# First attention: the key projection moved behind the output projection, PSUM banks reassigned, a head's weights split in two parts

## The chip, the cores and the metric

The kernel runs on one core of a Trainium2 chip. The metric is the time on the device in microseconds (us), lower is better. It is measured for the whole program, of which the part that the change touches is about two fifths.

## What is computed

The program computes two layers. Layer 0 is an attention with 32 query heads on 16 key heads (ALiBi bias, causal), times a gated network with experts; layer 1 is a recurrence, times an attention with experts. The change touches layer 0's attention alone:

```python
# x: 8 sequences of 512 tokens, 256 features; xn = layernorm(x)
qkv = inputs @ W_qkv                      # 32 query heads, 16 key and value heads of 64
k = jnp.repeat(k, NUM_QUERIES, axis=1)    # two query heads share a key head
scores = jnp.einsum('bhqd,bhkd->bhqk', q, k) / math.sqrt(HEAD_DIM)
scores = scores + bias[None]              # slope of the head times (key - query position)
scores = jnp.where(causal[None, None], scores, -jnp.inf)
attn = jax.nn.softmax(scores, axis=-1)
out = jnp.einsum('bhqk,bhkd->bhqd', attn, v)
return out.transpose(0, 2, 1, 3).reshape(B, S, Q_DIM) @ W_out
```

## The kernel before

`head_attention_phase` works in units. A unit is one key head with its two query heads on one sequence of 512 tokens; there are 16 heads of 8 sequences, 128 units, and they are numbered t, with head j outermost. Every engine has a program of its own, a loop over units written out by hand, and the programs meet through semaphores that count upward. Four blocks of 128 queries make up a unit; they are taken in the order 3, 0, 1, 2 and called 0 to 3 (`block_of`), so that step 0 has 512 keys, and steps 1, 2, 3 have 128, 256 and 384.

TensorE's `body(t)` (from L1060) is staggered over four units: it works on the scores of t+1, the turning (transposing) of the probabilities of t, the weighing of the values of t-1, and the projections of t+2. Its order is turn 0 (L1046), score 0 (L1034), turning of the values (L999), weighing (L1056), key and value projection of t+2 (L985), turns 1 and 2, scores 1 and 2, query projection of t+2 (L985), turn 3, score 3, and the output projection of t-1 (L1011) in two halves of three matmuls, m=1 and then m=0. The products are built from high and low parts, three terms each: high by high, low by high, high by low. A wait is put ahead of the last matmuls of the stage before (`last`, `late`), so that it is taken while others run.

There are eight PSUM banks: two for scores, two for turned probabilities, one for the weighed output, and three (`m_ps`) that the projections share. In body t with parity par, the keys and values go to bank par, the turned values of t+1 and then the queries of t+2 to bank 1-par, and the output projection's m=1 to bank 2 and m=0 to bank 1-par. So m=0 waits until VectorE's `q_rest` has read the queries there.

ScalarE takes the high parts out of PSUM (`take_k`, `take_v`, `take_q`, `take_o`), computes the exponentials (`exps`, L817) and copies half of each turned block (`turn_out`, L824). VectorE adds the bias and finds the maxima (`mask`, L902), inverts the sums (`invert`, L908), copies the other half (L914) and makes the low parts (`k_rest` L889, `values` L894, `q_rest` L882, `rest_o` L925); it sums the output into `acc` (`add_out`, L921), and at a head's last unit it makes the next head's two bias tiles (`set_bias`, L876). GpSimd scales the probabilities (`scale`, L769) and splits a head's raw weights in high and low part (`split`, L760 and L762). SP copies the keys to the other 64 partitions (`copy_k`, L712), and at a head's end issues a spill of x and the loads of the weights of the head after the next.

TensorE's loop runs over the 16 heads. In it stand two bodies, then an inner loop of two passes over two bodies, then two more bodies: six bodies of code for eight units. GpSimd's program is arranged likewise, with the split of the next head's weights ahead of the last two units.

Of the kernel before, what the change touches and what calls it, by code (L numbers as in the profile page):

```python
# [14 lines left out]
P = 128  # L15
B, S, D = 8, 512, 256
KT = D // P
TT = S // P
# [579 lines left out]
def head_attention_phase(nc, w_heads, wo_heads, slopes, ident, xh, xl, acc, xh_dram, xl_dram, row_sb, coef_sb,  # L598
# [9 lines left out]
    with ExitStack() as ctx:  # L608
# [57 lines left out]
        o_low = sem("at_o_low")  # L666
        zeroed = sem("at_zeroed")
        pool_ticks, dve_ticks, pe_ticks = sem("at_pool_ticks"), sem("at_dve_ticks"), sem("at_pe_ticks")
        block = ctx.enter_context(nc.Block())
# [18 lines left out]
        def kv_count(n):  # L688
            return n * 5 + (-3)

        def q_count(n):
            return n * 5 + (-2)

        def v_count(n):
            return n * 5 + 1

# [6 lines left out]
        def _(sp):  # L703
# [24 lines left out]
            with sp.Fori(0, KVH // 2) as jj:  # L728
                for jp in range(2):
                    j = jj * 2 + jp  # L730
                    with sp.Fori(0, PAIRS) as pair:
                        for par in range(2):
                            copy_k(kv_count(j * B + pair * 2 + (par + 2)), par)

                    to, half = ((xh_dram, xh), (xl_dram, xl))[jp]
                    sp.dma_start(to[:, :, ds(jj * S, S)], half[:, :, ds(jj * S, S)].bitcast(F32)).then_inc(spilled, 16)

                    sp.wait_ge(w_split, j + 1)
                    sp.wait_ge(wo_split, j + 1)
# [11 lines left out]
        def _(pool):  # L751
# [19 lines left out]
            def body(t):  # L771
                scale(t, 3)
                for j in range(3):
                    scale(t + 1, j)

            pool.wait_ge(w_loaded[0], 32)
            split(wh[:], wl[:], w_raw[0][:], 0).then_inc(w_split, 1)
            for j in range(3):
                scale(0, j)
            with pool.Fori(0, KVH // 2) as jj:  # L780
                for jp in range(2):
                    j = jj * 2 + jp
                    body(j * B)

                    pool.wait_ge(proj, j * (5 * B) + out_count(-1, 0))
                    wait_alone(pool, w_loaded[jp], jj * 32 + 32, pool_ticks)
                    split(woh[:], wol[:], wo_raw[jp][:], j * 2 + 1).then_inc(wo_split, 1)
                    body(j * B + 1)
                    with pool.Fori(1, PAIRS - 1) as pair:
                        for par in range(2):  # L790
                            body(j * B + pair * 2 + par)

                    pool.wait_ge(proj, j * (5 * B) + q_count(B - 1))
                    wait_alone(pool, w_loaded[1 - jp], (jj + jp) * 32 + 32, pool_ticks)
                    split(wh[:], wl[:], w_raw[1 - jp][:], j * 2 + 2).then_inc(w_split, 1)
                    body(j * B + (B - 2))
                    body(j * B + (B - 1))

        @block.scalar
        def _(act):  # L800
# [8 lines left out]

            def take_v(par):  # L810
                act.activation(vT[HD:P, :], m_ps[par][HD:P, :], ACT.Copy).then_inc(vT_out, 1)
# [21 lines left out]
            take_k(1, 0)  # L833
            take_v(0)
            take_q(2, 0)
            take_k(4, 1)
            take_v(1)
# [23 lines left out]
        def _(dve):  # L861
# [30 lines left out]
            def values(count, par):  # L892
                dve.wait_ge(proj, count)
                dve.tensor_copy(v[par][:].rearrange("p i d -> p (i d)"), m_ps[par][:, 0:TT * HD])\  # L894
                    .then_inc(proj_out, 1)
# [31 lines left out]
            def body(t, par, b_before, new_head=None):  # L927
# [19 lines left out]
                q_rest(t + 2, par)  # L947
# [3 lines left out]
                invert(t + 1, 2)  # L951
                add_out(t + (-1), 1 - par, b_before, 1)
                add_out(t + (-1), 1 - par, b_before, 0)

# [18 lines left out]
            for m in (1, 0):  # L973
                add_out(KVH * B - 1, 1, B - 1, m, skipped=3)

        @block.tensor
        def _(pe):
# [15 lines left out]
            def project_kv(n, par, b, last):  # L993
                project(m_ps[par], P, b, last)

            def turn_v(n, par):

                for i in range(TT):
                    ins = pe.transpose(m_ps[par][:, HD * i:HD * i + HD], vT[HD:P, P * i:P * i + P], ident[HD:P, HD:P])  # L999
                ins.then_inc(proj, 1)  # L1000

            def project_out(n, par, bank_free, last):

                for m in (1, 0):
# [3 lines left out]
                    for i, (w, o) in enumerate([(woh, oh), (wol, oh), (woh, ol)]):  # L1008
                        if m == 0 and i == 2:
                            last()  # L1010
                        ins = pe.matmul(bank[:], w[:, m * P:m * P + P], o[par][:], start=(i == 0), stop=(i == 2))  # L1011
                    ins.then_inc(proj, 1)
# [46 lines left out]

            def body(t, half, par, b_next, new_head=None, new_out=None):  # L1060

                def pair_turnable():
                    turnable(t, 1, 3)
                    pe.wait_ge(proj_out, v_count(t + 1))

                def next_turnable():
                    turnable(t, 3, 4)
                    pe.wait_ge(o_low, t + 1)

# [8 lines left out]
                if new_head is not None:  # L1078

                    pe.wait_ge(w_split, new_head + 1)  # L1080
# [12 lines left out]

            pe.wait_ge(zeroed, 1)
            pe.wait_ge(w_split, 1)
            project(m_ps[0], P, 0)
            project(m_ps[1], 0, 0)
            values_free(0)
            pe.wait_ge(proj_out, 1)
# [22 lines left out]
            pe.wait_ge(o_low, KVH * B + 1)  # L1122
            project_out(KVH * B - 1, 1, lambda: (pe.wait_ge(proj_out, 5 * KVH * B + 5), pe.wait_ge(vT_out, KVH * B + 2)), lambda: None)


# [1754 lines left out]
```

## Time and profile before

| | us |
|---|---|
| median of 3 runs | 3462.16 (3461.97 to 3463.49) |
| the profiled execution | 3461.67 |
| its span, first to last instruction | 3459.7 |
| of it, the first attention | about 62 to 1510 |

Busy time of the engines over the whole span: TensorE's matmuls 3203.6 us (93%), its weight loads 2347.7 (68%), VectorE 2336.1 (68%), ScalarE 2063.6 (60%), GpSimd 1184.1 (34%). The page has the engines' busy share in 40 slices, the DMA queues, and the costliest groups of instructions by line. A matmul's row gives its start and a modelled end that overlaps the next one, so that stages of TensorE are best measured from start to start. PE is TensorE, PEld its weight loads, DVE is VectorE, ACT is ScalarE, POOL is GpSimd. Register, branch and semaphore instructions have no rows.

### The profile page before, as it was taken

Reading aid. Unit: us, or ns where it says so; the run is one execution under the profiler, and the core shown is the slowest. Engines: PE = TensorE matmul, PEld = TensorE weight load, DVE = VectorE, ACT = ScalarE, POOL = GpSimd, SP = SyncE. Lnnn points to the kernel's source line nnn. Section 1 sums busy time; section 2 is a strip of 40 time slices with the busy share of each in tenths; the row PEclk is TensorE's granted clock in tenths of the full one; section 3 lists DMA queues with packets and bytes.
Section 4 is the critical chain, followed back from the end, with each engine's and each line's share of the span. In section 5 each row is a group of like instructions: output and inputs, shape, how many; then the busy total and the mean of one; then the engine's idle time right before and its main releaser. Section 6 shows DMA issues by size and latency. Waiting matters only on the chain. (4 is left out here: it accounts for less than half of the span.)

```text
span 3459.7 us, 72480 instructions
## 1 busy us (share of the span) xinstructions
PE 3203.6 (93%) x22702; PEld 2347.7 (68%) x22702; DVE 2336.1 (68%) x6854; ACT 2063.6 (60%) x4947; POOL 1184.1 (34%) x1820
## 2 busy tenths in 40 slices
PE   4999999999999999989999979879999964999995
PEld 3666666666666666668888855546666654888884
DVE  5788877877888788876666645556666625666665
ACT  4777777777777777765655543236566621555553
POOL 4444434443443344443333320042322202334432
PEclk9999999999999999999999989979999966999998
DMA  2111111111111111143433331101111134445545
GB/s 86 36 32 35 34 26 30 35 35 35 32 35 35 35 33 34 35 142 122 134 124 120 127 115 56 56 19 28 32 26 28 27 122 149 119 126 142 128 121 164
DMA packets 165548, 246.35 MB, mean 71 GB/s; under 512 B 30770, under 2 KB 115506, under 8 KB 165426
## 3 DMA queue, kind: packets, MB, share of 16 engines
q1 hardware_dynamic: 150834, 224.85, 21.2%
q0 software_dynamic: 14592, 19.93, 3.5%
q8 instruction: 69, 1.13, 0.1%
q14 instruction: 53, 0.43, 0.0%
HBM read 159.79 MB, written 41.16 MB: 58 GB/s over the span
## 5 line engine op out<-in xcount | busy, mean ns | idle before, releaser
L769 POOL TENSOR_SCALAR at_p<-at_p,at_recip 128x512 f32<-128x512 f32 (+3 forms) x1030 | 534.4, 535 | 865.5 <-DVE at_recip L908 865.5
L817 ACT ACTIVATE at_p<-at_p,at_nmax 128x512 f32<-128x512 f32 (+3 forms) x1032 | 571.6, 557 | 247.1 <-DVE at_nmax L902 235.8
L902 DVE CUSTOM_DVE_ANT_0 at_p<-at_s_ps,at_bias 128x512 f32<-128x512 f32 (+3 forms) x1032 | 449.1, 479 | 3.6 <-PE at_s_ps L1034 3.5
L1878 DVE CUSTOM_DVE_ANT_0 aa_a_ps<-aa_a_ps,aa_hidden 128x128 f32<-128x128 f32 (+3 forms) x512 | 247.3, 507 | 176.1 <-PE aa_a_ps L2042 172.9
L1034 PE MATMUL at_s_ps<-at_k_twice,at_q 64*128 64x512 f32 (+3 forms) x3096 | 343.4, 340 | 3.3 <-DVE at_nmax L902 3.3
L1056 PE MATMUL at_o_ps<-at_pT,at_v 128*64 128x512 f32 (+3 forms) x2064 | 307.5, 440 | 0.0
L1778 ACT ACTIVATE aa_pT<-aa_b_ps 128x512 f32<-128x512 f32 (+1 forms) x384 | 196.6, 529 | 178.8 <-PE aa_b_ps L2060 176.1
L1046 PEld LDWEIGHTS at_t_ps<-ident,at_p 64*128 64x128 f32 x5120 | 191.0, 138 | 143.2 <-issue 143.2
L914 DVE COPY at_pT<-at_t_ps 128x512 f32<-128x512 f32 (+3 forms) x512 | 235.9, 479 | 47.1 <-PE at_t_ps L1046 44.9
L526 DVE SCALAR_TENSOR_TENSOR nw_hl<-nw_h,nw_coef_now,nw_hh 128x512 fp32r<-128x512 f32 x192 | 149.9, 781 | 162.4 <-ACT nw_hh L454 162.4
L449 ACT ACTIVATE nw_h<-nw_h_ps,nw_b 128x512 f32<-128x512 f32 x192 | 132.2, 688 | 211.1 <-PE nw_h_ps L553 210.7
L1046 PE MATMUL at_t_ps<-ident,at_p 64*128 64x64 f32 x5120 | 241.7, 230 | 4.1 <-POOL at_p L769 3.2
L1056 PEld LDWEIGHTS at_o_ps<-at_pT,at_v 128*64 128x64 f32 x2064 | 137.0, 137 | 148.3 <-issue 121.1
L1034 PEld LDWEIGHTS at_s_ps<-at_k_twice,at_q 64*128 64x128 f32 x3096 | 226.7, 189 | 9.1 <-DVE at_nmax L902 3.9
L2593 POOL DMA_INDIRECT moe_dram<-ex_o,places x76 | 124.8, 1642 | 304.2 <-ACT ex_o L2620 212.1
L391 POOL TENSOR_SCALAR nw_w1h<-nw_w_raw 128x256 fp32r<-128x256 f32 x192 | 104.2, 543 | 324.1 <-PE nw_o_ps L568 318.4
L824 ACT ACTIVATE at_pT<-at_t_ps 128x512 f32<-128x512 f32 (+3 forms) x512 | 207.6, 431 | 2.4 <-PE at_t_ps L1046 2.3
L2042 PE MATMUL aa_a_ps<-aa_k,aa_q 128*128 128x128 f32 (+3 forms) x512 | 191.9, 387 | 14.9 <-DVE aa_nmax L1878 11.8
L985 PE MATMUL at_m_ps<-xh,at_wh 128*128 128x512 f32 (+1 forms) x520 | 189.5, 445 | 13.0 <-POOL at_wl L762 11.9
L817 ACT ACTIVATION_READ_ACCUMULATOR at_p<-at_p,at_nmax 128x1 f32 x1032 | 195.5, 189 | 0.0
L2632 ACT ACTIVATE ex_act<-ex_a_ps 128x512 f32<-128x512 f32 x114 | 68.1, 597 | 185.9 <-PE ex_b_ps L2728 185.9
L2685 DVE TENSOR_TENSOR ex_hid<-ex_act,ex_b_ps 128x512 f32<-128x512 f32 x114 | 78.5, 688 | 135.8 <-ACT ex_act L2632 134.6
(317 smaller groups left out, 8029.8 us busy)
## 6 DMA issues: line engine op xcount, KB each, us to landing
w_raw<-in_w_dram SPq DMA_DIRECT2D x57, 768.0 KB, 5.8
at_k_twice<-at_k_twice SPq DMA_DIRECT2D x130, 256.0 KB, 2.8
nw_w_raw<-in_w_all_dram SPq DMA_DIRECT2D x26, 1024.0 KB, 5.0
nw_w_raw<-in_w_all_dram SPq DMA_DIRECT2D x52, 512.0 KB, 6.9
nw_xh<-xh_dram SPq DMA_DIRECT2D x10, 512.0 KB, 4.2
nw_xl<-xl_dram SPq DMA_DIRECT2D x10, 512.0 KB, 4.9
at_w_raw<-in_w_heads_dram SPq DMA_DIRECT2D x18, 256.0 KB, 3.8
nw_x<-in_x_dram SPq DMA_DIRECT2D x9, 512.0 KB, 5.9
```

The source lines that it names most:

```text
L769: pool.tensor_scalar(p, p, recip[:, u:u + 1], 1.0, ALU.mult, ALU.mult).then_inc(scaled, 1)
L817: act.activation(p_sb[:, u, 0:N], p_sb[:, u, 0:N], ACT.Exp, bias=nmax[:, u:u + 1], scale=-1.0, accum_out=total[:, u:u + 1]).then_inc(exped, 1)
L824: act.activation(pT[par][:, :, 0:qt + 1, qt * P + HD:qt * P + P], turned_half(1)[:, :, turned_at(j), :], ACT.Copy).then_inc(odd_out, 1)
L902: dve.tensor_tensor_reduce(out=p_sb[:, u, 0:N], in0=s_ps[u % 2][:, score_at(u // 2)], in1=bias[:, u % 2, S - N:S], scale=1.0, scalar=BIG, ...
L914: dve.tensor_copy(pT[par][:, :, 0:qt + 1, qt * P:qt * P + HD], turned_half(0)[:, :, turned_at(j), :])\
L985: ins = pe.matmul(bank[:], weight[:, k, w:w + P], x[:, k, ds(b * S, S)], start=(i == 0 and k == 0), stop=(i == 2 and k == KT - 1))
L1034: ins = pe.matmul(s_ps[h][:, score_at(j)], qst[par][rows, q, at], k_twice[par][rows, k, 0:N], start=(i == 0), stop=(i == 2))
L1046: ins = pe.transpose(turned_half(half)[:, h, turned_at(j).start + k, :], p_sb[rows, 2 * j + h, k * P:k * P + P], ident[rows, rows])
L1056: ins = pe.matmul(o_ps[HD * h:HD * h + HD, k * P:S], v[par][:, k, :], pT[par][:, h, k, k * P:S], start=(k == 0), stop=(k == TT - 1))
L1778: act.activation(pT[group_of(n, s) % 2][:, s % REP, piece * S:piece * S + N], b_ps[done % 3][:, 0:N], ACT.Exp, scale=-1.0)\
L1878: dve.tensor_tensor_reduce(out=a_ps[i % 2][:, 0:N], in0=a_ps[i % 2][:, 0:N], in1=hidden[:, S - N:S], scale=1.0, scalar=BIG, op0=ALU.add, o ...
L2042: pe.matmul(a_ps[i % 2][:, 0:N], q_all[n % 2][:, head // 2, N - P:N], k_all[n % 2][:, head % 2, g, 0:N], start=True, stop=True).then_inc(s ...
```

## The change

TensorE projects the keys and values three units ahead in place of two, and does it as the last stage of the body, directly behind the output projection; the weighing is followed by turn 1. One more such projection stands in the prologue. The banks are given out anew: the turned values go to bank 2, the output projection's m=0 to bank par (which ScalarE has emptied with `take_v`), and the keys and values of t+3 to bank 1-par behind the queries of t+2. ScalarE takes the keys first in its body and the values behind a wait of their own, for the values' turning. VectorE makes the keys' low part ahead of `values`, and the output's low part behind `invert(t + 1, 0)`. The next head's weights are split in two parts, keys and values first, queries a unit later, and the two users wait for one part each. TensorE's eight bodies of a head are written out in its loop, without an inner loop; GpSimd's inner loop has one body.

```diff
@@ counts
         def kv_count(n):
-            return n * 5 + (-3)
+            return n * 5 + (-4)
         def v_count(n):
-            return n * 5 + 1
+            return n * 5 + 2
@@ sync
-                    sp.wait_ge(w_split, j + 1)
+                    wait_alone(sp, w_split, 2 * j + 2, sp_ticks)
@@ gpsimd
+            def split_heads(raw, part, n):
+                at = slice(part * P, part * P + P)
+                split(wh[:, :, at], wl[:, :, at], raw[:, :, at], n).then_inc(w_split, 1)
...
-                    body(j * B + 1)
-                    with pool.Fori(1, PAIRS - 1) as pair:
-                        for par in range(2):
-                            body(j * B + pair * 2 + par)
-                    pool.wait_ge(proj, j * (5 * B) + q_count(B - 1))
+                    with pool.Fori(1, B - 3) as b:
+                        body(j * B + b)
+                    pool.wait_ge(proj, j * (5 * B) + kv_count(B - 1))
                     wait_alone(pool, w_loaded[1 - jp], (jj + jp) * 32 + 32, pool_ticks)
-                    split(wh[:], wl[:], w_raw[1 - jp][:], j * 2 + 2).then_inc(w_split, 1)
+                    split_heads(w_raw[1 - jp], 1, j * 3 + 3)
+                    body(j * B + (B - 3))
+                    wait_alone(pool, proj, j * (5 * B) + q_count(B - 1), pool_ticks)
+                    split_heads(w_raw[1 - jp], 0, j * 3 + 4)
                     body(j * B + (B - 2))
                     body(j * B + (B - 1))
@@ scalar
-            def take_v(par):
+            def take_v(count, par):
+                act.wait_ge(proj, count)
                 act.activation(vT[HD:P, :], m_ps[par][HD:P, :], ACT.Copy).then_inc(vT_out, 1)
...
+                    take_k(kv_count(t + 2), par)
                     turn_out(t, 0, par)
+                    take_v(v_count(t + 1), par)
                     exps(t + 1, 0)
                     exps(t + 1, 1)
                     take_o(t, 1 - par)
-                    take_k(kv_count(t + 2), par)
                     turn_out(t, 1, par)
                     turn_out(t, 2, par)
-                    take_v(par)
@@ vector
                 mask(t + 1, 1)
+                k_rest(t + 2, par)
                 dve.wait_ge(summed, t + 1)
                 values(v_count(t + 1), 1 - par)
-                rest_o(t, 1 - par)
-                k_rest(t + 2, par)
...
                 invert(t + 1, 0)
+                rest_o(t, 1 - par)
                 turn_out(t, 3, par)
@@ tensor
                 turn(0)
-                score(t + 1, 1 - par, 0, lambda: values_free(t + 1))
+                score(t + 1, 1 - par, 0, values_turnable)
                 turn_v(t + 1, 1 - par)
-                weigh(t + (-1), 1 - par, lambda: pe.wait_ge(proj_out, out_count(t + (-2), 0)))
-                project_kv(t + 2, par, b_next, pair_turnable)
+                weigh(t + (-1), 1 - par, lambda: turnable(t, 1, 3))
                 turn(1)
                 turn(2)
                 score(t + 1, 1 - par, 1)
                 score(t + 1, 1 - par, 2)
-                project_q(t + 2, par, b_next, next_turnable)
+                project_q(t + 2, par, (b + 2) % B, lambda: turnable(t, 3, 4))
                 turn(3)
                 score(t + 1, 1 - par, 3)
-                project_out(t + (-1), 1 - par, lambda: pe.wait_ge(proj_out, q_count(t + 2)), next_unit)
+                project_out(par, lambda: pe.wait_ge(o_low, t + 1), lambda: pe.wait_ge(vT_out, t + 3),
+                            lambda: pe.wait_ge(proj_out, q_count(t + 2)))
+                project_kv(t + 3, par, (b + 3) % B, next_unit)
...
             project(m_ps[1], P, 1)
-            pe.wait_ge(proj_out, 3)
             project(m_ps[0], 0, 1)
+            pe.wait_ge(proj_out, 5)
+            project(m_ps[0], P, 2)
...
             with pe.Fori(0, KVH) as j:
-                body(j * B, j * PAIRS, 0, 2)
-                body(j * B + 1, j * PAIRS, 1, 3, new_out=j)
-                with pe.Fori(1, PAIRS - 1) as pair:
-                    for par in range(2):
-                        body(j * B + pair * 2 + par, j * PAIRS + pair, par, pair * 2 + (par + 2))
-                body(j * B + (B - 2), j * PAIRS + (PAIRS - 1), 0, 0, new_head=j + 1)
-                body(j * B + (B - 1), j * PAIRS + (PAIRS - 1), 1, 1)
+                for b in range(B):
+                    body(j * B + b, j * PAIRS + b // 2, b % 2, b, j + 1 if b == B - 3 else None,
+                         j + 1 if b == B - 2 else None, j if b == 1 else None)
```

## Rows read from the trace of the kernel before

**Rows 1.** Busy time by engine in the first attention; columns in the header.
```profile
core 0: us, PE busy (x) PEld busy (x) DVE busy (x) ACT busy (x) POOL busy (x), PEclk, DMA share, GB/s
75.00:1490.00 1415.00, 1414.15 (x12946) 950.17 (x12946) 1132.45 (x3837) 1056.34 (x3046) 571.82 (x1076) 1.00 0.14 33
```

**Rows 2.** Who waited for whom there: us in total, times, longest.
```profile
PEld at_m_ps L1011 <- DVE at_q L882: 24.1, 113, 0.2
```

**Rows 3.** TensorE's matmuls in one unit by time: start, us, engine, line, tiles.
```profile
709.50 0.71 PE L1046 MATMUL at_t_ps<-ident,at_p 64*128 64x64 f32 x16
...
713.44 0.73 PE L985 MATMUL at_m_ps<-xh,at_wh 128*128 128x512 f32 x2
...
715.04 0.59 PE L1046 MATMUL at_t_ps<-ident,at_p 64*128 64x64 f32 x12
...
717.89 0.59 PE L1046 MATMUL at_t_ps<-ident,at_p 64*128 64x64 f32 x12
...
718.98 0.50 PE L1011 MATMUL at_m_ps<-at_oh,at_woh 128*128 128x512 f32 x1
719.32 0.40 PE L1011 MATMUL at_m_ps<-at_oh,at_wol 128*128 128x512 f32 x1
...
719.78 0.44 PE L1011 MATMUL at_m_ps<-at_oh,at_woh 128*128 128x512 f32 x1
720.06 0.40 PE L1011 MATMUL at_m_ps<-at_oh,at_wol 128*128 128x512 f32 x1
...
720.62 0.28 PE L1046 MATMUL at_t_ps<-ident,at_p 64*128 64x64 f32 x2
```

**Rows 4.** The values' turning, once a unit, at a head's steps.
```profile
699.69 0.40 PE L999 MATMUL at_m_ps<-ident,at_vT 64*128 64x64 f32 x4
...
733.04 0.40 PE L999 MATMUL at_m_ps<-ident,at_vT 64*128 64x64 f32 x4
...
744.29 0.40 PE L999 MATMUL at_m_ps<-ident,at_vT 64*128 64x64 f32 x4
...
777.64 0.40 PE L999 MATMUL at_m_ps<-ident,at_vT 64*128 64x64 f32 x4
...
788.85 0.34 PE L999 MATMUL at_m_ps<-ident,at_vT 64*128 64x64 f32 x3
```

**Rows 5.** Other engines in the unit of rows 3, by time.
```profile
715.15 0.59 ACT L808 ACTIVATE at_k_twice<-at_m_ps 64x512 fp32r<-64x512 f32 x1 [0.99 <-PE at_m_ps L985]
...
718.99 0.68 DVE L882 SCALAR_TENSOR_TENSOR at_q<-at_m_ps,at_q 128x512 fp32r<-128x512 f32 x1
...
720.68 1.27 DVE L921 TENSOR_TENSOR acc<-at_m_ps,acc 128x512 f32 x2
```

**Rows 6.** VectorE's bias tiles for a new head, by time.
```profile
1490.71 1.11 DVE L876 TENSOR_SCALAR at_bias<-at_rel,at_slope 128x512 f32<-128x512 f32 x2
```

**Rows 7.** The prologue, by time: first scores, and the low part of unit 1's queries.
```profile
62.32 0.96 PE L1034 MATMUL at_s_ps<-at_k_twice,at_q 64*128 64x512 f32 x6
...
63.06 0.69 DVE L882 SCALAR_TENSOR_TENSOR at_q<-at_m_ps,at_q 128x512 fp32r<-128x512 f32 x1 [0.72 <-ACT at_q L804]
```

**Rows 8.** Whole program, DMA queue of TensorE's code: packets, MB, share of 16 engines.
```profile
q8 instruction: 69, 1.13, 0.1%
```

**Rows 9.** The same queue, 75 to 165 us.
```profile
q8 instruction: 5, 0.08, 0.4%
```

**Rows 10.** All DMA queues, 165 to 1500 us.
```profile
q1 hardware_dynamic: 17638, 44.66, 13.9%
q14 instruction: 2, 0.02, 0.0%
```

**Rows 11.** Busy time by engine from 80 to 165 us; columns as in rows 1.
```profile
80.00:165.00 85.00, 85.00 (x794) 57.57 (x793) 68.73 (x235) 64.47 (x187) 34.58 (x66) 1.00 0.15 36
```

**Rows 12.** One packet of that queue, 80 to 90 us.
```profile
q8 instruction: 1, 0.02, 0.7%
```

**Rows 13.** DMA issues of the whole program: times, KB each, median us to landing.
```profile
at_wo_raw<-in_wo_heads_dram SPq DMA_DIRECT2D x18, 128.0 KB, 3.8
...
recip_dram<-aa_recip SPq DMA_DIRECT2D x32, 8.0 KB, 1.4
```

More of the change, by code:

```diff
@@ L667, in head_attention_phase @@
         zeroed = sem("at_zeroed")
+        sp_ticks = sem("at_sp_ticks")
         pool_ticks, dve_ticks, pe_ticks = sem("at_pool_ticks"), sem("at_dve_ticks"), sem("at_pe_ticks")
@@ L774, in body @@
                     scale(t + 1, j)
+            def split_heads(raw, part, n):
+                at = slice(part * P, part * P + P)
+                split(wh[:, :, at], wl[:, :, at], raw[:, :, at], n).then_inc(w_split, 1)
             pool.wait_ge(w_loaded[0], 32)
-            split(wh[:], wl[:], w_raw[0][:], 0).then_inc(w_split, 1)
+            for part in range(2):
+                split_heads(w_raw[0], part, part)
             for j in range(3):
@@ L786, in _ @@
                     wait_alone(pool, w_loaded[jp], jj * 32 + 32, pool_ticks)
-                    split(woh[:], wol[:], wo_raw[jp][:], j * 2 + 1).then_inc(wo_split, 1)
-                    body(j * B + 1)
-                    with pool.Fori(1, PAIRS - 1) as pair:
-                        for par in range(2):
-                            body(j * B + pair * 2 + par)
-                    pool.wait_ge(proj, j * (5 * B) + q_count(B - 1))
+                    split(woh[:], wol[:], wo_raw[jp][:], j * 3 + 2).then_inc(wo_split, 1)
+                    with pool.Fori(1, B - 3) as b:
+                        body(j * B + b)
+                    pool.wait_ge(proj, j * (5 * B) + kv_count(B - 1))
                     wait_alone(pool, w_loaded[1 - jp], (jj + jp) * 32 + 32, pool_ticks)
-                    split(wh[:], wl[:], w_raw[1 - jp][:], j * 2 + 2).then_inc(w_split, 1)
+                    split_heads(w_raw[1 - jp], 1, j * 3 + 3)
+                    body(j * B + (B - 3))
+                    wait_alone(pool, proj, j * (5 * B) + q_count(B - 1), pool_ticks)
+                    split_heads(w_raw[1 - jp], 0, j * 3 + 4)
                     body(j * B + (B - 2))
@@ L833, in _ @@
             take_k(1, 0)
-            take_v(0)
+            take_v(1, 0)
             take_q(2, 0)
             take_k(4, 1)
-            take_v(1)
+            take_v(4, 1)
             take_q(5, 1)
@@ L893, in values @@
                 dve.wait_ge(proj, count)
-                dve.tensor_copy(v[par][:].rearrange("p i d -> p (i d)"), m_ps[par][:, 0:TT * HD])\
+                dve.tensor_copy(v[par][:].rearrange("p i d -> p (i d)"), m_ps[2][:, 0:TT * HD])\
                     .then_inc(proj_out, 1)
@@ L951, in body @@
                 invert(t + 1, 2)
-                add_out(t + (-1), 1 - par, b_before, 1)
-                add_out(t + (-1), 1 - par, b_before, 0)
+                add_out(t + (-1), par, b_before, 1)
+                add_out(t + (-1), par, b_before, 0)
             set_bias(0, True, 2)
@@ L973, in _ @@
             for m in (1, 0):
-                add_out(KVH * B - 1, 1, B - 1, m, skipped=3)
+                add_out(KVH * B - 1, 0, B - 1, m, skipped=2)
         @block.tensor
@@ L993, in project_kv, with project_out @@
             def project_kv(n, par, b, last):
-                project(m_ps[par], P, b, last)
+                project(m_ps[1 - par], P, b, last)
             def turn_v(n, par):
                 for i in range(TT):
-                    ins = pe.transpose(m_ps[par][:, HD * i:HD * i + HD], vT[HD:P, P * i:P * i + P], ident[HD:P, HD:P])
+                    ins = pe.transpose(m_ps[2][:, HD * i:HD * i + HD], vT[HD:P, P * i:P * i + P], ident[HD:P, HD:P])
                 ins.then_inc(proj, 1)
-            def project_out(n, par, bank_free, last):
+            def project_out(par, o_ready, bank_free, last):
                 for m in (1, 0):
@@ L1008, in project_out @@
                     for i, (w, o) in enumerate([(woh, oh), (wol, oh), (woh, ol)]):
-                        if m == 0 and i == 2:
-                            last()
-                        ins = pe.matmul(bank[:], w[:, m * P:m * P + P], o[par][:], start=(i == 0), stop=(i == 2))
+                        if i == 2:
+                            (o_ready if m else last)()
+                        ins = pe.matmul(bank[:], w[:, m * P:m * P + P], o[1 - par][:], start=(i == 0), stop=(i == 2))
                     ins.then_inc(proj, 1)
@@ L1058, in weigh, with body, values_turnable @@
                 ins.then_inc(summed, 1)
[L1060 to L1068, printed above, removed]
+            def body(t, half, par, b, new_keys=None, new_queries=None, new_out=None):
+                def values_turnable():
+                    values_free(t + 1)
+                    pe.wait_ge(proj_out, out_count(t + (-2), 1))
                 def next_unit():
@@ L1074, in body @@
                 turn(0)
-                score(t + 1, 1 - par, 0, lambda: values_free(t + 1))
+                score(t + 1, 1 - par, 0, values_turnable)
                 turn_v(t + 1, 1 - par)
-                weigh(t + (-1), 1 - par, lambda: pe.wait_ge(proj_out, out_count(t + (-2), 0)))
-                if new_head is not None:
-                    pe.wait_ge(w_split, new_head + 1)
-                project_kv(t + 2, par, b_next, pair_turnable)
+                weigh(t + (-1), 1 - par, lambda: turnable(t, 1, 3))
                 turn(1)
@@ L1085, in body @@
                 score(t + 1, 1 - par, 2)
-                project_q(t + 2, par, b_next, next_turnable)
+                if new_queries is not None:
+                    pe.wait_ge(w_split, new_queries * 2 + 2)
+                project_q(t + 2, par, (b + 2) % B, lambda: turnable(t, 3, 4))
                 turn(3)
@@ L1091, in body @@
                     pe.wait_ge(wo_split, new_out + 1)
-                project_out(t + (-1), 1 - par, lambda: pe.wait_ge(proj_out, q_count(t + 2)), next_unit)
+                project_out(par, lambda: pe.wait_ge(o_low, t + 1), lambda: pe.wait_ge(vT_out, t + 3),
+                            lambda: pe.wait_ge(proj_out, q_count(t + 2)))
+                if new_keys is not None:
+                    pe.wait_ge(w_split, new_keys * 2 + 1)
+                project_kv(t + 3, par, (b + 3) % B, next_unit)
             pe.wait_ge(zeroed, 1)
-            pe.wait_ge(w_split, 1)
+            pe.wait_ge(w_split, 2)
             project(m_ps[0], P, 0)
@@ L1098, in _ @@
             values_free(0)
-            pe.wait_ge(proj_out, 1)
             turn_v(0, 0)
@@ L1113, in _ @@
             with pe.Fori(0, KVH) as j:
-                body(j * B, j * PAIRS, 0, 2)
-                body(j * B + 1, j * PAIRS, 1, 3, new_out=j)
-                with pe.Fori(1, PAIRS - 1) as pair:
-                    for par in range(2):
-                        body(j * B + pair * 2 + par, j * PAIRS + pair, par, pair * 2 + (par + 2))
-                body(j * B + (B - 2), j * PAIRS + (PAIRS - 1), 0, 0, new_head=j + 1)
-                body(j * B + (B - 1), j * PAIRS + (PAIRS - 1), 1, 1)
+                for b in range(B):
+                    body(j * B + b, j * PAIRS + b // 2, b % 2, b, j + 1 if b == B - 3 else None,
+                         j + 1 if b == B - 2 else None, j if b == 1 else None)
             weigh(KVH * B - 1, 1)
-            pe.wait_ge(o_low, KVH * B + 1)
-            project_out(KVH * B - 1, 1, lambda: (pe.wait_ge(proj_out, 5 * KVH * B + 5), pe.wait_ge(vT_out, KVH * B + 2)), lambda: None)
+            pe.wait_ge(proj_out, 5 * KVH * B + 5)
+            pe.wait_ge(o_high, KVH * B + 1)
+            project_out(0, lambda: pe.wait_ge(o_low, KVH * B + 1), lambda: None, lambda: None)
 RH = D // HD
```

## The prediction

> **What bounds the kernel now.** I read the page by engine first, then the busy times of the stage that the change touches, then who waits there, then one unit instruction by instruction, and last the instruction queues among the DMA rows. The first attention fills the 1415 us from 75 to 1490 us, and in it TensorE is busy 1414.15 us while VectorE has 1132, ScalarE 1056 and GpSimd 572 [rows 1]. So a wait of another engine costs nothing here until it reaches TensorE. What the reader is to see is that the only wait for a value that recurs on TensorE is 0.2 us of a weight load behind VectorE's q rest, 113 times [rows 2]. The rest of a unit is the matmuls' own issue, and the gaps between stages in it.
>
> One unit is 720.62 - 709.50 = 11.12 us [rows 3]. A head of eight units is 788.85 - 699.69 = 89.16 us, against 8 x 11.12 = 88.94: two of the eight steps are longer, 744.29 - 733.04 = 11.25 (the back edge of the inner pair loop) and 788.85 - 777.64 = 11.21 (the head's edge) [rows 4].
>
> **The steady unit.** In a run of equal 128x128 matmuls the starts are 0.23 us apart (two steps from 719.32 to 719.78) [rows 3]. The key projection alone, six such matmuls between the weighing and the second turn, takes 715.04 - 713.44 = 1.60 us [rows 3]. Six times 0.235 is 1.41. The other 0.19 is paid at its two ends: the first matmul after another tile shape stands 0.34 from the next (718.98 to 719.32 shows the same), and the last one gives way 0.1 late. In the new order it follows the output projection, of the same shape, so the front gap goes; its back gap is the one that the output projection had before turn 0; and the weighing now meets turn 1 directly, for which I take the price of weighing to projection. Gain 0.19 us a unit. The trace has no row of weighing followed by a turn: bounds 0.10 us better or worse than that.
>
> The second half of the output projection now writes the bank that the keys left early in the unit and no longer the one that q rest is reading. Its first matmul stood 720.06 - 719.78 = 0.28 from the second where 0.235 is the rule [rows 3], so 0.05 us goes (bounds 0 and 0.05). The wait for q rest is now two matmuls later and is what is late next. With everything after the weighing 1.6 us earlier, turn 3 begins 6.8 us into the unit; q rest ran 718.99 to 719.67, that is, it began 1.1 us after turn 3's start of 717.89 [rows 3, 5], so it ends at 8.6 if it starts as long after turn 3 as before, and the matmul behind the wait is due at 9.1. Half a microsecond covers it.
>
> The other moved steps, each with its cover. ScalarE takes the keys first in the unit; they are ready 0.1 us after turn 0 begins, and behind this wait stands the copy of turn 0, not ready before 0.7: the 0.59 us of the take [rows 5] fit between. The value take then waits for the value turn (done at 1.8) with the exponentials behind it; the first of these needed its mask, at 2.3, and slips to 2.4, and TensorE asks for it only a unit later. VectorE's key rest and values lie between masks 1 and the turn copies, in an idle of 1 us that the trace has there. The low half of the output is now made after invert 0 and ends at 7.2; the projection wants it at 8.3. The sums into acc took 1.27 us and began 1.69 us after q rest did [rows 5]: they end at 10.9, and VectorE's next step waits until 0.7 us into the next unit. The wait before the first score for the bank of those sums is met 0.7 us early. SP's key copy is issued 3.3 us sooner and takes 2.8 us of the 7 that it has; SP's spill and weight loads behind it move with it. So TensorE stays the bound, at 11.12 - 0.19 - 0.05 = 10.88 us: 8 x 0.24 = 1.9 us a head.
>
> **The head.** The eight unit bodies stand one after the other in TensorE's loop, where it had six, two of them run twice. The inner edge goes: 0.13 us. At the head's edge VectorE's two new biases took 1.11 us ahead of its first turn copy [rows 6]; in the new unit that slips by about 0.5 us with 2 us to spare, so 0.09 goes too. GpSimd splits a head's weights in two parts of half the size: keys and values when the last unit's keys are projected, 7 us before they are used; queries 3 us before. Both are covered by the rest of the unit, and what is delayed behind them is a scale with over 3 us of slack. SP's changed wait counts the same event. Together 1.9 + 0.13 + 0.09 = 2.12 us a head, 34 us in 16.
>
> **The prologue** gets a third key projection behind q rest of unit 1. The first score began at 62.32; q rest began 63.06 and took 0.69 [rows 7], and the six matmuls take 1.6: the score begins at 65.4, 3.1 us later, once (bounds 1.5 and 3.5, as the tail of the last unit may give some back). Gain so far 34 - 3 = 31 us.
>
> **What the longer loop costs.** The instruction queue q8 moves TensorE's code in pieces: 69 packets and 1.13 MB over the program, 16.4 KB each [rows 8]. Five come in the stretch in which the six bodies run for the first time [rows 9], and none from 165 to 1500 us, where q14, that of the other engines, is the only one of the two to move anything, though the loop is run fifteen times more [rows 10]. So the 82 KB or so of the loop stay where the engine reads them; and since TensorE is busy for all of the 85 us in which the five come [rows 11], a piece is fetched ahead of its need. [...] Eight bodies are 8/6 x 82 = 109 KB and touch eight pieces, for the loop begins and ends inside one; the piece ahead is the ninth. I expect the loop's first piece to be gone when the back edge wants it, at each of 15 edges, and TensorE to wait for a fetch. No row has such a wait. Below it is bounded by the packet's own time, 1.1 us (0.7% of 16 engines in 10 us) [rows 12], or nothing if the piece is held; above by the 3.8 us in which 128 KB came from HBM to this stage; a short write landed in 1.4 [rows 13]. [...] 15 x 3.0 = 45 us.
>
> [...]
>
> **Sum.** Profiled execution 3461.67 (its span 3459.7 and 2.0 around it; the median of the three runs is 3462.16, 0.5 more). 3461.7 - 31 + 45 = 3475.7.
>
> **Rivals.**
> 1. *The code is held.* For it: no loop here was ever fetched twice. Against: none here is nearly as long. Then 3461.7 - 31 = 3431; with the bounds of the gaps (0.1 us x 128 = 13 us) 3420 to 3445. Chance 0.25. This is the one on the other side; it decides from the point where eight pieces and the one ahead fit.
> 2. *Fetched again but cheaply*, 1.1 to 2.0 us an edge, nearer the packet's own time: 15 x 1.5 = 23, 3454. Chance 0.12.
> 3. *A wait takes the place of the gaps*: q rest late by over the 0.5 us that I leave it, say 0.2 a unit, or weighing to turn dearer; the unit stays 11.1. With the fetches 3461.7 + 3 - 4 + 45 = 3506, without 3461. Chance 0.05.
> The forecast, 2.0 to 4.0 us an edge, has 0.58: 3461 to 3491.
>
> **How the numbers follow.** Likeliest 3475.7. The range takes in rival 1 down to 3428, a little under its centre, and the dearest fetch, 3492; what is left out is the lower half of rival 1, a tenth, and rival 3 with fetches and a still dearer one, under a tenth. By signs (this kernel's measurement tells 0.2%, 7 us, from no change): faster is rival 1, half of rival 2: 0.31; same is the other half and fetches of 2.0 to 2.5 us: 0.19; slower is the rest: 0.50. The forecast's own range is 3461 to 3491.
>
> **What would show it.** Key projection directly behind the output projection, unit starts 10.88 us apart; no idle of the weight load behind q rest; head edges as steps of 13 to 15 us (10.9 if rival 1 holds); q8 packets all through the stage, at least one a head, in place of none. It is wrong if the packets don't come, or come without a halt of TensorE.

## The result, and the profile after

| | before | after |
|---|---|---|
| median (range), 20 runs each | 3461.64 us (3459.08 to 3464.12) | 3467.31 us (3463.04 to 3472.47) |
| the profiled execution | 3461.67 | 3465.64 |
| its span | 3459.7 | 3463.9 |

The ratio is 1.0017, interval 1.0010 to 1.0024: 5.7 us slower, inside the 0.2% that I called no change. The forecast was 3475.7, a loss of 14 us, with 3428 to 3492 as its range. The measured loss is less than half of that, and the interval shows that it is a loss.

The whole-program rows of the kernel after, engine (busy, share, instructions) and the queue of TensorE's code (packets, MB, share):

```profile
PE 3177.8 (92%) x22708; PEld 2371.3 (68%) x22708; DVE 2362.2 (68%) x6854; ACT 2092.8 (60%) x4947; POOL 1189.6 (34%) x1854
...
q8 instruction: 205, 3.36, 0.4%
```

TensorE's matmuls have 26 us less busy time than before, in a program that takes 4 us more. The code queue has 205 packets in place of 69 [rows 8]. From 165 to 1500 us, where q8 had none [rows 10], it now has these:

```profile
q8 instruction: 133, 2.18, 0.7%
...
q14 instruction: 2, 0.02, 0.0%
```

That is 133 / 15 = 8.9, nine pieces of 16.4 KB for each pass of the loop. Busy time by engine of almost the same stretch as rows 1, columns as there, and the wait in it that is new (total, times, longest):

```profile
75.00:1480.00 1405.00, 1376.10 (x12842) 964.36 (x12843) 1149.68 (x3802) 1074.78 (x3017) 574.17 (x1102) 1.00 0.15 35
...
PE at_t_ps L1055 <- issue: 28.7, 15, 2.2
```

TensorE was hardly idle there before (0.85 us in 1415). Now it idles 28.9 us, and 28.7 of them are fifteen waits ahead of a turn (L1055 is what L1046 was), put down to its own issue and not to another engine. The wait of rows 2, VectorE's q rest, has no row any more. The cause stands in the rows of the loop's branch, which TensorE's sequencer works ahead of its matmuls; shortest, median and longest in ns. Before, then after:

```profile
L1113 PEldq COMPARE_BRANCH  x16: 67/209/222, 163.2 to 1500.3; - x16
```
```profile
L1122 PEldq COMPARE_BRANCH  x16: 83/3671/3922, 163.3 to 1502.6; - x16
```

The shortest of the sixteen is the one that leaves the loop. A branch back cost 0.2 us and costs 3.7. Around the first of them, at 163.3 us, TensorE's matmuls were (start, us, line, tiles; in brackets the idle time ahead):

```profile
163.60 0.63 PE L994 MATMUL at_m_ps<-xh,at_wh 128*128 128x512 f32 x2
164.07 0.63 PE L994 MATMUL at_m_ps<-xh,at_wl 128*128 128x512 f32 x2
164.54 0.63 PE L994 MATMUL at_m_ps<-xl,at_wh 128*128 128x512 f32 x2
167.10 0.71 PE L1055 MATMUL at_t_ps<-ident,at_p 64*128 64x64 f32 x16 [1.93 <-issue]
```

The branch begins at 163.3 and the work queued ahead of it runs until about 165.0 (its last matmul starts at 164.77): that hides 1.7 us of it, and the rest is the halt. A whole unit of after, a head's first:

```profile
703.37 0.71 PE L1055 MATMUL at_t_ps<-ident,at_p 64*128 64x64 f32 x16 [2.18 <-issue]
703.86 0.97 PE L1043 MATMUL at_s_ps<-at_k_twice,at_q 64*128 64x512 f32 x6
704.67 0.40 PE L1008 MATMUL at_m_ps<-ident,at_vT 64*128 64x64 f32 x4
705.01 2.37 PE L1065 MATMUL at_o_ps<-at_pT,at_v 128*64 128x512 f32 x16
707.31 0.59 PE L1055 MATMUL at_t_ps<-ident,at_p 64*128 64x64 f32 x12
...
711.25 0.50 PE L1020 MATMUL at_m_ps<-at_oh,at_woh 128*128 128x512 f32 x1
711.59 0.40 PE L1020 MATMUL at_m_ps<-at_oh,at_wol 128*128 128x512 f32 x1
711.83 0.39 PE L1020 MATMUL at_m_ps<-at_ol,at_woh 128*128 128x512 f32 x1
712.06 0.40 PE L1020 MATMUL at_m_ps<-at_oh,at_woh 128*128 128x512 f32 x1
712.29 0.40 PE L1020 MATMUL at_m_ps<-at_oh,at_wol 128*128 128x512 f32 x1
712.53 0.39 PE L1020 MATMUL at_m_ps<-at_ol,at_woh 128*128 128x512 f32 x1
712.76 0.63 PE L994 MATMUL at_m_ps<-xh,at_wh 128*128 128x512 f32 x2
...
714.25 0.46 PE L1055 MATMUL at_t_ps<-ident,at_p 64*128 64x64 f32 x8
```

714.25 - 703.37 = 10.88 us, where rows 3 have 11.12. The weighing meets turn 1 after 707.31 - 705.01 = 2.30, what it took to the projection before; the six output matmuls and the projection behind them are 0.23 to 0.24 apart without a break.

### The profile page after: what moved, and what is told of

The parts are those of the page before. It is cut to its first block and busy times, and to the rows that moved or that the text cites. A ratio compares the mean times of both kernels' runs of the same rounds, so it can differ in the third digit from the quotient of the medians.

```text
span 3463.9 us, 72142 instructions
## 1 busy us (share of the span) xinstructions
PE 3177.8 (92%) x22708; PEld 2371.3 (68%) x22708; DVE 2362.2 (68%) x6854; ACT 2092.8 (60%) x4947; POOL 1189.6 (34%) x1854
## 5 line engine op out<-in xcount | busy, mean ns | idle before, releaser
L911 DVE CUSTOM_DVE_ANT_0 at_p<-at_s_ps,at_bias 128x512 f32<-128x512 f32 (+3 forms) x1032 | 462.3, 488 | 62.7 <-PE at_s_ps L1043 44.5
L1055 PEld LDWEIGHTS at_t_ps<-ident,at_p 64*128 64x128 f32 x5120 | 189.6, 138 | 149.6 <-issue 149.6
L1055 PE MATMUL at_t_ps<-ident,at_p 64*128 64x64 f32 x5120 | 241.8, 230 | 31.9 <-issue 28.7
L994 PE MATMUL at_m_ps<-xh,at_wh 128*128 128x512 f32 x522 | 177.3, 420 | 14.8 <-POOL at_wl L763 12.4
```

What stands on the lines that cost most here:

```text
L911: dve.tensor_tensor_reduce(out=p_sb[:, u, 0:N], in0=s_ps[u % 2][:, score_at(u // 2)], in1=bias[:, u % 2, S - N:S], scale=1.0, scalar=BIG, ...
L1055: ins = pe.transpose(turned_half(half)[:, h, turned_at(j).start + k, :], p_sb[rows, 2 * j + h, k * P:k * P + P], ident[rows, rows])
```

## The experiments

TensorE's program was counted in instructions, from its start: after's loop of eight bodies is the 1752 at places 302 to 2053, and the trace has 1752 of its instructions from branch to branch. A packet of 16,384 bytes, a piece, is taken as 256 instructions. That is an estimate: where the code runs straight on in new_order_sixteen, the trace has 255 instructions to a packet (twelve packets in a row). Of the kernel before, a median of 3461.2 to 3461.5 us was measured beside each group of runs; each figure below has its ratio to that.

**Is it the length of the loop or the order of the stages?** Two kernels have one part of the change each. The first is before, with only its eight bodies written out:

```diff
-                body(j * B, j * PAIRS, 0, 2)
...
+                for b in range(B):
+                    body(j * B + b, j * PAIRS + b // 2, b % 2, (b + 2) % B, j + 1 if b == B - 2 else None,
+                         j if b == 1 else None)
```

> The kernel before, with TensorE's eight bodies of a head written out and nothing else changed. Theory of the fetch (the back edge of a loop of eight bodies meets code that is no longer held; its branch takes 3.3 to 3.9 us, and TensorE halts for that less what was queued ahead of the branch, which in the old order is about 0.3 us): 69 packets of code become about 205, the head's step becomes 11.2 + 3.3 = 14.5 us, and the time is 3462 - 2 (inner edges gone) + 15 x 3.3 = 3509 us. Rival of a fixed price (a halt of 2.0 us whatever the order): 3490 us. Rival that the halts come from the new order or the split weights and not from the code's length: no halts, 3460 us.

Measured 3558.81 us, ratio 1.028 (1.0266 to 1.0294). Its branch, and one head's edge:

```profile
L1113 PEldq COMPARE_BRANCH  x16: 83/4344/5058, 163.4 to 1597.2; - x16
```
```profile
545.96 0.40 PE L1011 MATMUL at_m_ps<-at_ol,at_woh 128*128 128x512 f32 x1
550.52 1.12 PE L1046 MATMUL at_t_ps<-ident,at_p 64*128 64x64 f32 x16 [4.16 <-issue]
551.36 1.66 PE L1034 MATMUL at_s_ps<-at_k_twice,at_q 64*128 64x512 f32 x6
...
553.38 3.42 PE L1056 MATMUL at_o_ps<-at_pT,at_v 128*64 128x512 f32 x16
```

The length alone costs 97 us, twice the 48 that I had for it. Only TensorE's code differs from before, and q8 has 205 packets in place of 69: q8 carries that code. Three things are more than in after: the branch takes 4.3 us; only 0.3 us of work is queued at it, since this order has no projection behind the output projection; and behind every halt the granted clock is 0.5 for 6.8 us (the weighing takes 3.42 where it takes 2.37 at full clock). Per head that is 4.2 us of halt and 2.4 of half clock: 15 x 6.6 = 99, less the 2 of the inner edges. By the mechanism the expectation was right, by the price it missed widely.

The second is after, with six bodies of code:

```diff
-                for b in range(B):
...
+                body(j * B, j * PAIRS, 0, 0)
+                body(j * B + 1, j * PAIRS, 1, 1, new_out=j)
+                with pe.Fori(1, PAIRS - 1) as pair:
...
+                body(j * B + (B - 2), j * PAIRS + (PAIRS - 1), 0, B - 2, new_queries=j + 1)
+                body(j * B + (B - 1), j * PAIRS + (PAIRS - 1), 1, B - 1)
```

> The changed kernel, with TensorE's loop laid out as before: two bodies, an inner loop of two passes over two bodies, two bodies. The order of stages, banks and the split of the weights stay as changed. Theory of the fetch: 69 packets, no halt at a head, units 10.89 us apart, inner edges of 0.1 us back; the time is 3467 - 33 (halts and clock) + 2 = 3436 us. Rival that the halts come from the new order or the split weights: they stay, 3467 us.

Measured 3430.46 us, ratio 0.991 (0.9896 to 0.9923), the loop's branch:

```profile
L1122 PEldq COMPARE_BRANCH  x16: 67/209/225, 163.4 to 1469.8; - x16
```

And its DMA queues, 165 to 1475 us:

```profile
q1 hardware_dynamic: 18000, 45.23, 14.3%
q14 instruction: 2, 0.02, 0.0%
```

No packet of q8 there, no halt, and every step from unit to unit is 10.89 us, at the inner edge and at the head's as well. So the order of the stages brings 31 us after the dearer prologue, and writing out the eight bodies takes 37 back.

**Does the halt go with the number of passes?** After, with two heads written out in the loop, so that it has 7 edges back in place of 15:

```diff
+            with pe.Fori(0, KVH // 2) as jj:
+                for jp in range(2):
+                    j = jj * 2 + jp
```

> The changed kernel, with two heads (sixteen bodies) written out in TensorE's loop, so that it has 7 back edges in place of 15. Theory that only the edge halts and straight code is fetched for free: 7 halts of 2.0 us, packets about as many as with eight bodies (14 or 15 a pass of two heads), 3467 - 8 x 2.0 - 1 = 3450 us. Rival that the fetching as such costs (each piece a little): 3465 us or more.

Measured 3450.41 us, ratio 0.9965 (0.9951 to 0.9978):

```profile
L1122 PEldq COMPARE_BRANCH  x8: 83/3634/3891, 249.6 to 1489.2; - x8
...
PE at_t_ps L1055 <- issue: 13.4, 7, 2.2
```

Seven halts of the same size as after's fifteen (1.9 us each by this row): sixteen bodies cost no more at an edge than eight, and only the jump back costs. Straight on, the pieces come ahead of their use: q8 has 182 packets, and the row of these halts has seven (eight_padded_less below has an exception).

**Is it a matter of pieces?** Instructions that wait for what is long true were put ahead of the loop. 215 of them move it to places 517 to 2268, where it touches seven pieces in place of eight; nothing else changes.

```diff
+            for _ in range(430):
+                pe.wait_ge(even_out, 1)
```

(In the trace the 430 waits are 215 instructions.)

> The changed kernel, with 215 waits that are met at once put ahead of TensorE's part of the attention, while it waits for the first weights; they move the loop of 1752 instructions from places 302 to 2053 of its program to 517 to 2268. Theory that eight pieces of 256 instructions are held, the one ahead among them: the loop now begins just behind the start of a piece (the packets' times put the starts at multiples of 256 less 0 to 30) and touches seven, and with the one ahead it fits: 69 to 72 packets, no halts, 3467 - 33 + 3 (the waits take 11 us where 8 are free) = 3437 us. Rival that the loop is too long wherever it lies, or that its halts have another cause: packets about 205, 3467 to 3470 us.

Measured 3445.53 us, ratio 0.9955 (0.9942 to 0.9969). Branch, and a head's edge:

```profile
L1124 PEldq COMPARE_BRANCH  x16: 76/208/238, 178.7 to 1485.1; - x16
```
```profile
528.32 0.63 PE L994 MATMUL at_m_ps<-xl,at_wh 128*128 128x512 f32 x2
528.88 0.71 PE L1055 MATMUL at_t_ps<-ident,at_p 64*128 64x64 f32 x16
```

71 packets and no halt, with the very same eight bodies. The waits themselves put TensorE's first projection from 53.65 to 69.16 us, which is why it isn't at new_order_six's time (the expectation had them cheaper). With 155 of them (310 in the line above) the loop stands at places 457 to 2208 and touches eight pieces again:

> As the padded kernel (3445.5 us, no halts), with 155 waits in place of 215 ahead of TensorE's loop. The loop of 1752 instructions then lies at places 457 to 2208, and begins 30 to 55 instructions ahead of the start of a piece. Theory of eight pieces: it touches eight again, with the one ahead nine, so each edge halts: 205 packets, and 3445.5 - 7 (60 waits of 0.12 us fewer) + 33 = 3471 us. Rival that the waits, or a later start of the loop, keep the halts away by themselves: 3438 us, 70 packets.

Measured 3541.36 us, ratio 1.0226 (1.0212 to 1.0240):

```profile
549.68 0.63 PE L994 MATMUL at_m_ps<-xl,at_wh 128*128 128x512 f32 x2
552.17 0.56 PE L1055 MATMUL at_t_ps<-ident,at_p 64*128 64x64 f32 x11 [1.85 <-issue]
555.16 0.48 PE L1055 MATMUL at_t_ps<-ident,at_p 64*128 64x64 f32 x5 [2.44 <-issue]
...
PE at_t_ps L1055 <- issue: 62.4, 30, 2.9
```

Sixty waiting instructions fewer cost 96 us. Eight pieces halt and seven don't, as forecast; the time missed the expectation by 70 us. Not foreseen: there are two halts at each edge, and the clock falls to half behind each pair. The loop begins with 30 to 55 instructions left in its first piece, TensorE is through them after eleven turns, and the next piece has only been asked for. The rows of q8 fit this: at each of the fifteen edges a packet starts 0.5 to 1.1 us after TensorE's restart, and the second halt ends 2.2 to 2.7 us after that start. No row names the piece that a packet holds, so that much stays my reading.

**What makes the branch 4.3 us in one kernel and 3.7 in the other?** In old_order_eight SP's spill of x and the loads of the next weights were issued 1.1 to 2.9 us ahead of the branch and moved data until some 3 us past its start; in after they were issued 2.7 to 4.6 us ahead of it. The spill and loads were put ahead of SP's last two key copies:

```diff
-                    with sp.Fori(0, PAIRS) as pair:
+                    with sp.Fori(0, PAIRS - 1) as pair:
...
+                    for par in range(2):
+                        copy_k(kv_count(j * B + (B - 2 + par + 2)), par)
```

> The kernel before with eight bodies written out (3559 us: a halt of 4.1 to 5.2 us at each head, and a stretch at half the clock of TensorE behind each), and SP's spill and loads of a head moved ahead of the key copies of the last two units, 20 us before the edge. Theory that the spill and the loads lie in the DMA queues when the code is asked for, and lengthen the fetch: the branch takes 3.4 to 3.7 us in place of 4.3, the halt comes down to 3.5, and if the clock then stays up at most heads, 3500 to 3520 us; if it still falls each time, 3540. Rival that the longer fetch has to do with the order alone: 3559 us.

Measured 3537.57 us, ratio 1.0222 (1.0208 to 1.0236):

```profile
L1115 PEldq COMPARE_BRANCH  x16: 83/3460/3882, 164.9 to 1575.9; - x16
...
PE at_t_ps L1048 <- issue: 48.9, 15, 3.6
```

The branch drops from 4.34 to 3.46 us, so other transfers at that moment lengthen the fetch by 0.9. It is the start of the code's packet that they put off: by the medians it comes 2.1 us after the branch's start in old_order_eight and 1.0 us after it here, and the packet itself takes about 1 us in both. The clock still fell behind 13 of the 15 halts, nine times for 3.4 us in place of 6.8. The same edit to after:

> The changed kernel, with the same move of SP's spill and loads. There the spill and the loads are over shortly before the edge and the branch takes 3.3 to 3.9 us. Theory of the DMA queues: little traffic to avoid, branch 3.3 to 3.6 us, 3461 to 3466 us. Rival that nothing of the halt is traffic: 3467 us.

Measured 3465.37 us, ratio 1.001 (1.0001 to 1.0019), branch median 3.53 us: its loads hardly lay in the way. The times can't tell the theory's 3461 to 3466 from the rival's 3467.

**What is the shorter wait for q rest worth?** In new_order_six, the output projection's m=0 was made to wait for q rest again, as before:

```diff
-                project_out(par, ..., lambda: pe.wait_ge(vT_out, t + 3),
+                project_out(par, ..., lambda: (pe.wait_ge(vT_out, t + 3), pe.wait_ge(proj_out, q_count(t + 2))),
```

> The changed kernel with six bodies, and the wait for the low part of the queries put back ahead of the first matmul of the output projection's second half, where the kernel before had it (the bank itself stays the new one). Theory that this wait was worth 0.05 us a unit: units of 10.93 us, 3430.5 + 128 x 0.05 = 3437 us. Rival that it was hidden and all of the gain came from the shapes of the stages: units of 10.89, 3430.5 us.

Measured 3438.83 us, ratio 0.9934 (0.992 to 0.9947):

```profile
709.96 0.44 PE L1020 MATMUL at_m_ps<-at_oh,at_woh 128*128 128x512 f32 x1
710.24 0.40 PE L1020 MATMUL at_m_ps<-at_oh,at_wol 128*128 128x512 f32 x1
```

The 0.28 us of rows 3 are back, and 8.4 us with them by the medians. The traces give the price of a unit better: its median step is 10.933 us for new_order_six's 10.887, so 0.05, and over the loop 5.7 us. The rest of the 8.4 is within the spread of the runs. The same edit in after itself was meant to tell whether less is queued at the branch with it:

> The changed kernel with its eight bodies, and the wait for the low part of the queries ahead of the output projection's second half, as before. With six bodies this wait costs 8 us. Theory that TensorE halts for the branch's 3.7 us less the work that its sequencer had queued by then (1.7 us in the changed kernel, since nothing stops the sequencer in the last stages; with the wait some 1.1): halts of 2.6 us in place of 2.0, so 3467 + 8 + 15 x 0.6 = 3484 us, and perhaps 1.6 us more for each further fall of the clock. Rival of a halt that doesn't depend on what is queued: 3475 us.

Measured 3471.61 us, ratio 1.0029 (1.0018 to 1.0039):

```profile
PE at_t_ps L1055 <- issue: 26.3, 15, 1.9
```

The halt is 1.8 us, not longer: the wait stands nine matmuls ahead of the branch (three of the output projection, six of the keys' and values'), and the sequencer has caught up again by then, with 1.77 us queued at the branch. My expectation fell and its rival came close.

**The prologue.** In new_order_six, the projection of unit 2's keys was put behind the first scores:

```diff
-            pe.wait_ge(proj_out, 5)
-            project(m_ps[0], P, 2)
...
+                if j == 0:
+                    pe.wait_ge(proj_out, 5)
+                    project(m_ps[0], P, 2)
```

> The changed kernel with six bodies, and in the prologue the third key projection behind the first scores of unit 0, in a pause of TensorE, in place of ahead of them. Theory that it stands on the path at 3 us there: 3427.5 us. Rival that the masks and exponentials of unit 0 set the end of the prologue anyway: 3430.5 us.

Measured 3428.84 us, ratio 0.9908 (0.9893 to 0.9923). The first score begins at 63.67 us in place of 65.95. Against new_order_six it is 1.6 us by the medians, whose ranges overlap, so its size stays open; it is the best of the versions measured.

## Why the prediction was right and where it was wrong

**The bound and the steady unit: right.** TensorE stayed the bound, and a unit went from 11.12 to 10.88 us, the figure of the forecast. Of its two parts, the bank of m=0 was put at 0.05 us, and six_q_wait has 0.046; the gap of the stage shapes is then 0.19, as taken. The weighing meets a turn for the same 2.30 us, so the bound of 0.10 either way wasn't needed. No moved step came late: no wait of TensorE for another engine recurs.

**The head and the prologue: nearly right.** New_order_six shows this gain without the halts. By its branch rows a head takes (1469.8 - 163.4) / 15 = 87.09 us, where before takes (1500.3 - 163.2) / 15 = 89.14: 2.05 us a head for the 2.12, or 33 in 16. From the first value turn in the loop to the last the traces have 1384.5 us for 1416.4, a gain of 32. Its first score began at 65.95 us, 3.6 later than in rows 7 (3.1 foreseen, 3.5 the bound; of it 0.4 us is a later start of the first projection, 53.59 for 53.21), and the first value turn in the loop 3.2 later (77.54 for 74.33). The 31.0 us by the medians fit this within their spread. The inner edge and VectorE's biases cost nothing any more, as worked out.

**The code: the mechanism right, its step mis-sized.** "I expect the loop's first piece to be gone when the back edge wants it" holds. That nine pieces, the one ahead among them, don't fit was my estimate, for no row of the kernel before shows how many are held. These runs fit eight held, the one ahead among them: with seven touched there is no halt (eight_padded, 71 packets), with eight there is (eight_padded_less, 206 packets, and after, 205). That the new loop touches eight was stated without its place. It is 1752 / 256 = 6.8 pieces long and touches seven or eight by where it begins, eight in most places; here the guess held. A jump back is not enough for a fetch: new_order_six jumps back over six pieces, fifteen times, without a packet and with a branch of 0.21 us.

The step that failed is the 3.0 us of "15 x 3.0 = 45 us". No run shows that term: it was my estimate, 3.3 us of branch less some 0.3 us of work queued ahead of it. In its place after has a branch of 3.68 us, 1.73 us of work queued and a halt of 1.98. The 0.3 is the queue of the old order: there a single output matmul is left at the branch, as old_order_eight shows (0.23 us from its branch to the end of its work, halt 4.2). In the new order the six matmuls of a projection stand behind the output projection, and 1.73 us of work is queued. The old order has a wait for q rest three matmuls ahead of the branch; in eight_q_wait that wait stands nine ahead, and 1.77 us is queued. That the place of the waits sets the queue is my reading, and which wait of the old order holds its sequencer back no run separates. The change that makes the fetch also hides half of it, and I carried the old figure over. The fetch itself was underestimated: I took 3.3 us in all, and the branch took 3.7, near the upper bound that I took from rows 13 (3.8). Where the code is read from, no row shows. Per edge, worked out from the rows of branches and matmuls (medians for branch and queue; the halt is the mean step from the last matmul ahead of the edge to the first turn behind it, less the 0.33 us of that step elsewhere):

| | branch, us | work queued | halt |
|---|---|---|---|
| forecast | 3.3 | 0.3 | 3.0 |
| after | 3.68 | 1.73 | 1.98 |
| new_order_sixteen | 3.78 | 1.73 | 1.99 |
| eight_padded_less, first halt | 3.45 | 1.73 | 1.82 |
| old_order_eight | 4.38 | 0.23 | 4.24 |
| old_eight_early_loads | 3.46 | 0.28 | 3.33 |

So 15 x 1.98 = 29.7 us stand where 45 was forecast. A second term was missing: behind two of the fifteen halts the clock fell, for 1.6 us more each, together 3.3. In the trace of after the stretch from first to last value turn grew from 1416.4 to 1417.3 us; without halts and clock it is 1417.3 - 29.7 - 3.3 = 1384.3, a gain of 32.1 for the 34 of the sum. The sum as measured is 3461.7 - 32 + 3 + 33 = 3465.7, against 3465.64 in the profiled execution. All of the miss of 10 us is the one term (45 for 33), less 2 in the gain. New_order_six bears this out: without halts and falls its trace has 1384.5 us where this working has 1384.3.

**The rivals.** The price came out on the border of rival 2 (1.1 to 2.0 us an edge) and not in the forecast's 2.0 to 4.0. Rival 1 is false for this kernel and yet true 215 instructions further on; I had taken it to depend on the loop's length alone, but it also depends on where the loop begins. After's loop reaches into its eighth piece with some twenty instructions (an estimate from its last place, 2053, and the packets' times).

## What to carry to other kernels

Count a loop's instructions on each engine and the pieces that it touches; where the jump back found its code held, q8 was silent (new_order_six: no packet, a branch of 0.2 us), and where it didn't, the branch's own row was microseconds long (after: nine packets a pass, 3.7 us). Its price on the engine was that row less the work already queued, behind which it hides (3.68 less 1.73 us in after, for a halt of 1.98), and that queue has to be read in the new order, not the old. A stage put behind another of the same tile shape saved the price of its joints, here 0.2 us a unit, and it can be had without unrolling: six bodies of code and the new order give 3430 us, 0.9% under before.

## What the runs showed of the hardware that I had not expected

**A halt can cost nearly as much again behind it.** In after, TensorE had idled 2.1 us when the following came, the granted clock at half for 3.4 us of it (start, us):

```profile
523.60 0.71 PE L1055 MATMUL at_t_ps<-ident,at_p 64*128 64x64 f32 x16 [2.13 <-issue]
...
525.41 3.83 PE L1065 MATMUL at_o_ps<-at_pT,at_v 128*64 128x512 f32 x16
```

And by stretches, this unit and the next (columns as in rows 1):

```profile
523.60:534.20 10.60, 10.60 (x95) 6.89 (x96) 7.13 (x23) 6.64 (x19) 2.50 (x4) 0.84 0.13 28
534.20:547.50 13.30, 13.30 (x127) 9.41 (x127) 10.94 (x38) 10.26 (x29) 6.80 (x14) 1.00 0.09 20
```

The weighing takes 3.83 us in place of 2.37, the mean granted clock is 0.84, and the next stretch is back at 1.00. Behind halts of 2.0 us it fell to 0.5 in 2 of 15 cases in after and in 4 of 7 in new_order_sixteen, behind those of 3.3 us in 13 of 15 and behind those of 4.2 in all. In after a fall costs 1.6 us; in old_order_eight, where the clock is down for 6.8 us, of which some 5 are work, it costs about 2.4. Why some of the equal halts are followed by it and others not, stays open. That after's runs spread over 9 us where before's spread over 5 fits a number of falls that differs from run to run: the three slowest of the 20 have a mean granted clock of 0.957, all others 0.958 to 0.960. The falls themselves are known from the profiled executions alone.

**Transfers of other queues lengthened a code fetch:** the branch takes 3.5 us in old_eight_early_loads and 4.3 in old_order_eight.

**All of the loop is fetched again, not only the piece that was lost:** nine packets a pass in after, where the loop touches eight pieces, which with the piece ahead makes nine.
